# One language-model tower on one core: ten logit tiles of the last cross unit issued early, and feed-forward up-products put ahead of down-products

## The reference, cut to what matters

```python
spatial_out = _spatial_experts(_ln(x, ...), idx_s, ...)       # unit "S" of a sequence
temporal_out = _temporal_experts(_ln(x, ...), idx_t, ...)     # unit "T", causal
fused = _cross_mha(spatial_out, temporal_out, ...)            # unit "C": queries from S, keys from T
x = x + fused
h2 = _ln(x, norm_mlp_w, norm_mlp_b)
x = x + (gelu(h2 @ mlp_w1.T + mlp_b1) @ mlp_w2.T + mlp_b2)
...
h = h + x
```

## Time and profile before

| | us |
|---|---|
| median of 3 runs | 1644.18 (1644.1, 1644.18, 1648.24) |
| the profiled execution, its own time | 1643.73 |
| span of the profiled execution, first to last instruction | 1642.0 |
| mean granted clock | 0.95 |
| busy: PE, PEld, DVE, ACT, POOL | 1513.5, 662.1, 1221.4, 1129.2, 998.9 |

### The profile page before, as it was taken

The page is one execution under the profiler, slowest core; times in us unless marked ns, Lnnn a source line. Parts: engine busy times, 40 slices in busy tenths (PEclk is TensorE's granted clock), DMA queues, the critical chain, the costliest instruction groups (busy, mean ns, idle before and its releaser), DMA issues. The chain is left out here.

```text
span 1642.0 us, 37445 instructions
## 1 busy us (share of the span) xinstructions
PE 1513.5 (92%) x8694; PEld 662.1 (40%) x8694; DVE 1221.4 (74%) x3412; ACT 1129.2 (69%) x2201; POOL 998.9 (61%) x1359
## 2 busy tenths in 40 slices
PE   5779949899999999999999999999999999885998
PEld 1238823233333433333333333333333333212665
DVE  6868848489888887978888887978888897253442
ACT  5757733567887878787787878778787878723332
POOL 7704443756777776766777686776777684513443
PEclk9779957999999999999999999999999999957999
DMA  3311143644554654654564564564565552111221
GB/s 83 103 31 46 52 74 50 83 77 71 79 84 62 81 77 62 85 74 72 74 85 62 73 84 63 78 79 73 67 88 65 68 79 44 25 15 34 66 69 53
DMA packets 140020, 110.34 MB, mean 67 GB/s; under 512 B 22720, under 2 KB 134464, under 8 KB 139968
## 3 DMA queue, kind: packets, MB, share of 16 engines
q1 hardware_dynamic: 137920, 105.53, 43.4%
q0 software_dynamic: 2048, 4.20, 1.1%
HBM read 19.29 MB, written 8.39 MB: 17 GB/s over the span
## 5 line engine op out<-in xcount | busy, mean ns | idle before, releaser
L1153 ACT ACTIVATE probs<-psum 128x512 f32<-128x512 f32 (+3 forms) x1536 | 755.0, 548 | 225.7 <-PE psum L1268 215.0
L1053 DVE TENSOR_REDUCE mx_S<-psum 128x1 f32<-128x512 f32 x512 | 326.3, 681 | 48.6 <-PE psum L1248 47.6
L1053 DVE TENSOR_REDUCE mx_C<-psum 128x1 f32<-128x512 f32 x512 | 317.8, 676 | 45.3 <-PE psum L1248 45.3
L1049 DVE CUSTOM_DVE_ANT_0 psum<-psum,causal 128x128 f32<-128x128 f32 (+3 forms) x512 | 242.5, 509 | 98.1 <-PE psum L1248 95.5
L1248 PE MATMUL psum<-ks_S,qs_S 96*128 96x512 bf16 x512 | 197.6, 397 | 10.4 <-DMA ks_S<-parts_k 6.3
L1248 PE MATMUL psum<-ks_C,qs_C 96*128 96x512 bf16 x512 | 199.6, 398 | 4.6 <-DMA ks_C<-parts_k 1.4
L1268 PE MATMUL psum<-qs_C,ks_C 99*128 99x512 bf16 x512 | 189.3, 385 | 3.6 <-ACT probs L1153 3.2
L1268 PE MATMUL psum<-qs_S,ks_S 99*128 99x512 bf16 x512 | 190.5, 383 | 0.2
L934 POOL CAST parts_q<-f_q 128x512 bf16<-128x512 f32 x48 | 29.3, 610 | 226.7 <-ACT f_q L1144 226.2
L1248 PE MATMUL psum<-ks_T,qs_T 96*128 96x128 bf16 (+3 forms) x512 | 155.6, 306 | 1.6 <-DVE mx_S L1053 1.1
L1268 PE MATMUL psum<-qs_T,ks_T 99*128 99x256 bf16 (+3 forms) x512 | 152.1, 301 | 3.0 <-ACT probs L1153 1.7
(11 more groups left out here) (186 smaller groups left out, 2705.8 us busy)
## 6 DMA issues: line engine op xcount, KB each, us to landing
qs_S<-parts_q SPq DMA_DIRECT2D x96, 128.0 KB, 4.5
ks_S<-parts_k SPq DMA_DIRECT2D x96, 128.0 KB, 5.0
qs_T<-parts_q SPq DMA_DIRECT2D x96, 128.0 KB, 4.4
ks_T<-parts_k SPq DMA_DIRECT2D x96, 128.0 KB, 4.6
qs_C<-parts_q SPq DMA_DIRECT2D x96, 128.0 KB, 4.4
ks_C<-parts_k SPq DMA_DIRECT2D x96, 128.0 KB, 4.9
w_in_S<-in_s_in SPq DMA_DIRECT2D x16, 257.0 KB, 2.8
w_in_T<-in_t_in SPq DMA_DIRECT2D x16, 257.0 KB, 2.7
```

The lines of the kernel that those rows point to most:

```text
L1049: nc.vector.tensor_tensor_reduce(tile[:, 0:last_key], tile[:, 0:last_key], causal[:, T - last_key:T], 1.0, NEG, ALU.add, ALU.max, mx[kind] ...
L1053: nc.vector.tensor_reduce(mx[kind][:, n:n + 1], tile, AX_X, ALU.max, negate=True).then_inc(reduced, 1)
L1153: nc.scalar.activation(probs[:, group_place(kind, b, n // 4), n % 4, t0:T], psum[:, LOGITS + ring_place(kind, b, n, RC), t0:T], ACT.Exp, s ...
```

## The change

Two edits that do not touch each other.

1. In slot (16, 2), at steps 27 to 31, PE issues two logit tiles of the last cross unit ahead of the score of that step (tiles 0 and 1 at step 27, and so on to 8 and 9 at step 31), and ACT takes the exponentials of the same tiles at the same steps. In slot (17, 0) these ten tiles are left out.
2. In the feed-forward block PE's stage b becomes turn(b), up(b-2), down(b-3), and DVE finishes b-4 in place of b-3 in stage b.

```diff
+EARLY_AT, EARLY_TILES = 27, 10
...
+def early_tiles(i, slot, n):
+
+    if isinstance(i, int) and (i, slot) == (B, 2) and n >= EARLY_AT:
+        return range(2 * (n - EARLY_AT), 2 * (n - EARLY_AT) + 2)
+    return ()
+
+
+def issued_early(kind, b, n):
+
+    return kind == "C" and isinstance(b, int) and b == B - 1 and n < EARLY_TILES
...
                 def slot_program(i, slot):
-                    (kn, bn), _, (kb, bb), (ko, bo) = units(i, slot)
+                    (kn, bn), (ka, ba), (kb, bb), (ko, bo) = units(i, slot)
...
-                        if n >= LAG and exists(bb):
+                        if n >= LAG and exists(bb) and not issued_early(kb, bb, n - LAG):
                             exponential(kb, bb, n - LAG)
+                        for m in early_tiles(i, slot, n):
+                            exponential(ka, ba, m)
...
-                        if n >= LAG and exists(bb):
+                        if n >= LAG and exists(bb) and not issued_early(kb, bb, n - LAG):
                             logits(kb, bb, n - LAG)
+                        for m in early_tiles(i, slot, n):
+                            logits(ka, ba, m)
...
                     if exists(b - 1):
                         scale_shift(b - 1, 1 - odd)
-                    if exists(b - 3):
-                        finish(b - 3, 1 - odd)
+                    if exists(b - 4):
+                        finish(b - 4, odd)
...
                     if exists(b):
                         turn(b, odd)
+                    if exists(b - 2):
+                        up(b - 2, odd)
                     if exists(b - 3):
                         down(b - 3, 1 - odd)
-                    if exists(b - 2):
-                        up(b - 2, odd)
```

## The result

| | before | changed |
|---|---|---|
| median, us | 1644.47 (6 runs, 1644.09 to 1648.24) | 1632.20 (6 runs, 1630.77 to 1633.95) |
| ratio | | 0.9922, 95% interval 0.9909 to 0.9935 |
| profiled execution: time, span | 1643.73, 1642.0 | 1631.52, 1629.7 |

The change makes the kernel 0.8% faster, 12.3 us by the medians and 12.2 us by the two profiled executions. I had predicted 1635.0, within 1631.0 to 1638.5.

A forecast was written before the change was run, and what follows sets the result against it. PE was taken to bound the feed-forward block except where it waits for gelu, with the attention tail second. 1643.73 - 9.05 (feed-forward) - 0.0 (early tiles) = 1634.7, median 0.45 above, stated as 1635.0 us, range 1631.0 to 1638.5.

The forecast's parts named there:

- The forecast case: Whole kernel: feed-forward gains 9.05 us, early tiles about 0.0, giving 1635.0 us; chance 68%.
- The wait for gelu goes and PE is the bound: Feed-forward block: down no longer waits for gelu, leaving only PE's own issue; 9.05 us less.
- The size of a stage: Feed-forward block: 7.60 us for a stage with a turn, 7.11 without, against 8.08 each before.
- the 9.8 that I gave as an upper bound: Feed-forward block: the gain would be 9.8 us if the turn costs 0.43 us.
- Finish one stage back costs nothing: Feed-forward block, DVE: finishing b-4 in place of b-3 was costed at nothing.
- The 5.8 us to spare: Feed-forward block: finish and normalise take 1.8 us, the next turn comes after a 7.6 us PE stage, leaving 5.8.
- Early tiles give 0.0: Attention tail: time saved ahead of the weighing is given back by a second turn 4.3 us later; about 0.0 us.
- The clock rises in the early tiles: Rival, attention tail: clock rises during early tiles, three steps at 0.96 us not 1.28 gain 1.0 us; 1634.0, chance 10%.
- The early tiles lose: Rival, attention tail: clock falls in two PE waits of about 1 us, costing 4.0 us; 1639.0, chance 6%.
- The slower rival: Feed-forward block: the chain down, y, normalise, turn decides, 15.6 us more; 1659.8, chance 2%.

The follow-up runs named there:

- e1: Kernel before with only the feed-forward edit, attention as before: 1694.11 us against 1704.36 before, ratio 0.9934.
- e2: Kernel before with only the early logit tiles, feed-forward as before: 1704.13 us against 1704.36 before, ratio 0.9998.
- e3: Changed kernel with DVE's finish left at b-3, all else kept: 1728.68 us against 1704.36 for the kernel before, ratio 1.0142.
- e4: Changed kernel with the ten early tiles at steps 22 to 26 in place of 27 to 31: ratio to the kernel before 0.9957.
- e5: Changed kernel with six early tiles, not ten: one ahead of each of scores 29 to 31, three behind score 31; ratio to before 0.9912.
- e10: Changed kernel plus useless PE products: 34 before the output, 7 before score 0, one behind scores 0 to 26, six before tile 0; 1628.19 us, ratio 0.9905.
- e9: Changed kernel with six spread early tiles plus useless PE products: 34 before the output, 7 before score 0, one behind scores 0 to 28; 1628.37 us, ratio 0.9914.
- e12: Changed kernel with six spread early tiles in place of ten, run again: 1629.59 us against 1643.51 before, ratio 0.9913.
- e11: The changed kernel run again, unaltered: 1632.26 us against 1643.51 before, ratio 0.9933.
- e6: Changed kernel plus useless PE products: 32 ahead of the previous unit's last output, one behind each of scores 0 to 25; ratio to before 0.9931.
- e8: Changed kernel with six spread early tiles plus useless PE products ahead of the previous unit's last output and behind scores; ratio to before 0.9914.

## Why the prediction was right

**The forecast case came in**: feed-forward gains, early tiles give nothing, each shown by itself in e1 and e2. Point by point:

- **The wait for gelu goes and PE is the bound**: right; the chain has no idle PE left.
- **The size of a stage**: the step that failed. I had 7.60 and 7.11 us from starts in the earlier trace rows; measured are 7.44 and 7.01. The terms mis-sized are down, 3.57 us and not 3.67, and the turn, 0.44 and not 0.49. My 3.67 was the time of a down that had waited, and 0.10 of it is the restart behind the wait. The 0.49 too was that of a turn that had waited, 0.36 us for xs (1610.05 in the earlier trace rows); behind its waits in e3 the turn takes 0.48 (1602.36 to 1602.84). Thirteen stages of 0.16 and two of 0.10 are 2.3 us: 11.4 were gained, not 9.05. That is beyond the 9.8 that I gave as an upper bound, since the bound moved the turn alone. The better row was there: the one down before that followed its turn without a wait, at 1610.54 in the earlier trace rows, was followed by up 3.60 us later:

```profile
1614.14 3.60 PE L1520 MATMUL psum<-hT,w 128*128 128x512 f32 x8
```

- **Finish one stage back costs nothing**: right, and the move was needed (e3). The 5.8 us to spare were less, since normalise now takes 3.1 us and not 1.1 (below): in the stage shown there it ends at 1590.05, and the turn that needs it starts at 1593.62, 3.6 us later.
- **Early tiles give 0.0**: right to 0.1 us, and by the steps named. Predicted and measured behind score 0: tile 0 17.1 and 17.18, score 31 23.1 and 23.13, second turn 24.45 and 24.38, tile 16 30.1 and 29.92, tile 18 31.5 and 31.45. That the scores held up are what costs the gain is shown by e4 and e5; that the low clock makes the steps long, by e10.
- **The clock rises in the early tiles** (1634.0): not in this profile. It rose 23.3 us behind score 0, during the last score, too late to shorten a step. Stretches of the changed kernel:

```profile
1461.00:1465.00 4.00, 4.00 (x11) 1.35 (x10) 2.08 (x3) 3.42 (x7) 0.00 (x0) 0.50 0.00 0
1466.00:1472.00 6.00, 4.07 (x24) 0.83 (x23) 0.97 (x2) 3.68 (x8) 1.39 (x4) 1.00 0.02 3
```

PE's products were gapless from 1459.70 to that moment. That activity releases the throttle is what the Trainium skill says ("TensorE: Matmul & The Clock Gate", "What's actually happening"), and the trace agrees.

- **The early tiles lose** (1639.0): not in the changed kernel, where the clock stayed at 1.00 through both waits of about 1 us. It did happen in e4, whose clock fell 26.8 us behind score 0, in the wait of 1.40 us ahead of the second turn.
- **The slower rival** needs finish ahead of the next normalise; that is e3, at 1.0142.

The result passed the forecast by 2.8 us in the medians and by 3.2 us in the profiled execution (1631.52 against 1634.7). Of these 2.3 are the stage's size. The profile's 0.9 us ahead of the tail come from no step of the change, and their cause stays open; it is no more than executions of one kernel differ by. That this part fell in the same direction is luck.

## What to carry to other kernels

When a wait is taken out of a pipeline, cost the pieces by rows in which they already follow one another without a wait, since a row behind a wait holds its restart. Before work is put ahead in a queue, ask what stands behind it there and whom that releases: ten early tiles gave nothing, and six, at most one to a score, brought tile 18 forward by 2.5 to 2.9 us. Where one engine's order moves by a stage, its partner's must move with it: the same reordering of PE took 0.7% off with finish one stage back and put 1.4% on without.

## What the runs showed of the hardware that I had not expected

**DVE's normalisation and POOL's residual block each other.** In the changed kernel the four operations of normalise take 3.07 us in a stage; they took 1.11 in the earlier trace rows. (In the kernel before only the last stage with a turn shows it, with 1.23 and 1.43 us for two of the four.) For one stage, the tile xs first (count, then ns min/median/max, first and last start), then the timeline:

```profile
L1476 DVE TENSOR_SCALAR xs<-X,mv,rstd_t x4: 339/773/1428, 1587.0 to 1588.6; 128x128 f32<-128x128 f32 x4
```

```profile
1586.98 3.07 DVE L1476 TENSOR_SCALAR xs<-X,mv,rstd_t 128x128 f32<-128x128 f32 x4
...
1587.31 1.30 POOL L1451 TENSOR_TENSOR base<-h,X 128x512 f32<-128x512 f32 x1 [1.99 <-DVE y L1484]
1588.69 1.27 POOL L1454 TENSOR_TENSOR base<-base,b 128x512 f32<-128x512 f32 x1
```

Two of the four take 0.34 us as ever. The last starts at 1588.6 and takes 1.43, so it ends at 1590.05, 0.09 us behind POOL's second operation (1588.69 + 1.27 = 1589.96). The third, 1.21 us long, ends as shortly behind POOL's first, which itself takes 1.30, and 1.17 to 1.19 in every stage of the kernel before. Since finish has moved, normalise and base both start behind y. The Trainium skill ("SBUF — State Buffer", "SBUF: two separate sides") says that a GpSimd operation and a DVE operation in a mode that uses two ports take one shared port pair as an exclusive lock: the one that starts first has it for its whole instruction, and the other waits. In what they last the trace agrees: no speed is shared, one waits the other out. In the order it does not by the recorded starts, as the last xs is recorded 0.07 us ahead of the POOL operation that it outlasts. That the ports are the cause is the page's word; no run here sets it apart. It costs nothing here, as PE is the bound.

**The clock makes idle time cost more than its length.** In e3 the holes, 25.9 us in sum, cost 10.3 us beyond themselves. In e9 and e10 useless products in idle time brought tile 18 forward by 1.1 and 2.1 us against the same tiles without them (e12, e11). By the turn of stage 3 0.1 and 2.7 us were left of it, against 1.2 and 4.1 by the medians. In e6 and e8, where holes of 0.7 to 2.1 us were left around the output ahead of score 0, they did not bring tile 18 forward.
